# Interleaving the context products with the W products, and the products with A with the FFN products, in a gated cross-attention and FFN layer

## What is computed

```python
xn = layernorm(x);  xh, ch = heads(xn), heads(ctx)          # 4 heads of 128
Q, K, V = xh @ Wh, ch @ Wh, ch @ Wh                         # per head
scores = einsum("bshe,bthe->bhst", Q, K) / sqrt(128)
A = maximum(abs((scores * decay).sum(axis=0)), 1)           # summed over all 64 sequences
O = einsum("hst,bthe->bshe", A, V);  Y = groupnorm(O) * gamma + beta
x = x + tanh(g1) * ((relu(xn @ wg) * Y) @ wo)
h = layernorm(x)
x = x + tanh(g2) * ((silu(h @ gate.T * gs) * (h @ up.T * us)) @ down.T * ds)
```

## Time and profile before

| | |
|---|---|
| time, median of 3 runs | 1441.88 us |
| lowest, highest | 1441.26, 1445.92 us |
| span of the profiled execution (first to last instruction) | 1447.4 us |
| PE busy, of that span | 1420.4 us (98%) |
| DVE, ACT, POOL busy | 1043.3, 726.3, 735.3 us |
| mean granted TensorE clock | 0.998 of 2.4 GHz |
| first part, Z of group 1 to Z of group 15 | 34.1 to 311.7 us |
| FFN groups 0 to 7 | 360 to 1025 us |

### The profile page before, as it was taken

The page is one execution under the profiler, slowest core; times in us unless marked ns, Lnnn a source line. Parts: engine busy times, 40 slices in busy tenths (PEclk is TensorE's granted clock), DMA queues, the critical chain, the costliest instruction groups (busy, mean ns, idle before and its releaser), DMA issues.

```text
span 1447.4 us, 20320 instructions
## 1 busy us (share of the span) xinstructions
PE 1420.4 (98%) x7097; PEld 728.3 (50%) x7135; DVE 1043.3 (72%) x1562; ACT 726.3 (50%) x1145; POOL 735.3 (51%) x734
## 2 busy tenths in 40 slices
PE   8999999999999999999999999999999999999998
PEld 4666666665445544455444444444444444444443
DVE  7788998878477676766776677564867768768762
ACT  5566565554555635455463545534344444443442
POOL 5656769863564445444553554434137237137235
PEclk9999999999999999999999999999999999999999
DMA  8999898973878796987888897886383473572432
GB/s 275 344 336 306 292 317 318 343 251 130 276 204 263 227 276 206 260 276 210 248 274 237 264 243 222 247 252 164 112 228 115 124 224 122 139 218 98 139 109 89
DMA packets 372920, 324.96 MB, mean 225 GB/s; under 512 B 259280, under 2 KB 285264, under 8 KB 372816
## 3 DMA queue, kind: packets, MB, share of 16 engines
q1 hardware_dynamic: 355248, 291.63, 66.2%
q10 hardware_dynamic: 17568, 31.99, 6.2%
HBM read 209.14 MB, written 114.43 MB: 224 GB/s over the span
## 4 chain that ended last, share of the span: by engine, by line
PE 74%; DVE 10%; DMA 6%; SPq 3%; issue 3%; ACT 2%; POOL 2%; ACTq 0%; DVEq 0%; POOLq 0%
PE ps L2067 24%; PE po L2067 8%; PE pyb L1930 7%; PE ps L2074 7%; PE ptb L2074 5%; PE pyb L2074 5%; PE ps L1988 5%; PE po L1930 3%; PE pyb L2058 3%; PE ptb L2058 3%; DMA wy_scratch<-misc 2%; SPq L510 2%; DVE reg L1129 1%; PE ptb L2062 1%; PE pyb L2062 1%
## 5 line engine op out<-in xcount | busy, mean ns | idle before, releaser
L2067 PE MATMUL ps<-x2t,gate 128*128 128x512 f16 x704 | 166.6, 379 | 1.2 <-DVE tmp L1436 1.1
L1930 PE MATMUL pyb<-xnt,wgs 128*128 128x512 f16 x708 | 166.3, 380 | 1.4 <-DVE wgs L1153 1.3
L2067 PE MATMUL ps<-op,wbuf 128*128 128x512 f16 x704 | 166.3, 379 | 0.5 <-issue 0.5
L2067 PE MATMUL ps<-x2t,up 128*128 128x512 f16 x704 | 166.3, 379 | 0.0
L1800 POOL TENSOR_TENSOR p5b<-p5b,p1b 128x512 f32<-128x512 f32 x44 | 55.7, 1265 | 209.1 <-ACT p5b L860 209.1
L1816 POOL TENSOR_TENSOR hid<-tmp,hid 128x512 f16<-128x512 f32 x88 | 104.6, 1190 | 105.9 <-ACT hid L836 105.9
L2074 PE MATMUL ps<-down_first,hid 128*128 128x512 bf16 x683 | 152.4, 379 | 2.1 <-POOL hid L1816 0.8
L1811 POOL TENSOR_TENSOR hsp<-hall,hsp 128x640 f16<-128x640 f32 (+2 forms) x72 | 123.6, 1731 | 37.1 <-ACT hsp L887 37.1
L2067 PE MATMUL po<-op,wbuf 128*128 128x512 f16 x528 | 129.0, 379 | 0.6 <-DVE u2b L1383 0.6
L1436 DVE SCALAR_TENSOR_TENSOR tmp<-ps,colsb,tmp 128x512 f32<-128x512 f32 x88 | 65.4, 744 | 68.2 <-PE ps L2067 62.3
L1988 PE MATMUL ps<-reg 128*128 128x256 f32 x768 | 109.7, 294 | 4.3 <-DVE reg L1129 3.8
(11 more groups left out here) (218 smaller groups left out, 2764.2 us busy)
## 6 DMA issues: line engine op xcount, KB each, us to landing
wbuf<-ws_scratch SPq DMA_DIRECT2D x44, 896.0 KB, 5.0
xr<-in_x SPq DMA_DIRECT2D x62, 512.0 KB, 6.3
raw<-in_ctx_t SPq DMA_DIRECT2D x32, 512.0 KB, 5.6
v_scratch<-tmp ACTq DMA_DIRECT2D x64, 256.0 KB, 6.0
raw<-v_scratch SPq DMA_DIRECT2D x32, 512.0 KB, 6.6
x_scratch<-xr SPq DMA_DIRECT2D x32, 512.0 KB, 4.8
xr<-x_scratch SPq DMA_DIRECT2D x32, 512.0 KB, 5.9
raw<-w_scratch SPq DMA_DIRECT2D x31, 512.0 KB, 6.0
```

The lines of the kernel that those rows point to most:

```text
L1930: last = e.matmul(dst, lhs[a], rhs[b], start=(k == 0 and i == 0), stop=(k == n - 1 and i == 2))
L2067: last = e.matmul(dst, upper(wt), act[i], start=start, stop=stop and exact, skip_group_check=True)
```

## The change

In the first part the six matmuls of a half of v are followed, one by one, by six matmuls of a W tile. In groups 1 to 13 PE's order becomes v(4g, 0) alone, then v(4g+1, 0) with half of w(4g), v(4g, 1) with the other half, v(4g+1, 1) with half of w(4g+1), rows, v(4g+2, 0), v(4g+2, 1) and v(4g+3, 0) in the same way with the rest of w(4g+1) and with w(4g+2), and v(4g+3, 1) alone. Group 14 has three such halves. W tiles 4 to 56 with t % 4 under 2 go into the two `pz` banks, where Z has been. w(4g) therefore waits for z_lo(4g+2), w(4g+1) for z_lo(4g+3), and the next group's z for the w_out of these tiles. ACT's order is fitted to it. In the FFN's first eight groups the 12 matmuls of o(q), for q over 3 (28 pairs), each follow one of the first 12 matmuls of the step; their waits now stand at the step's start.

The numbers of matmuls, their operands, DVE's, POOL's and SP's programs and all DMAs stay the same in number and size.

```diff
         def pw(t):
+            if 4 <= t < LATE - 1 and t % 4 < 2:
+                return pz[t % 4]
             if t <= LATE:
                 return pyb[:, :]
...
(ACT, group g)
-                v_out(4 * g)
-                v_out(4 * g + 1)
+                if more and g < NG - 2:
+                    v_out(4 * g)
+                    w_out(4 * g)
+                    v_out(4 * g + 1)
...
                 ct_hi(g + 1, 1)
                 if g < NG - 2:
-                    w_out(4 * g)
+                    w_store(4 * g)
                 x_hi(2 * g + 3, 0)
-                if g < NG - 2:
-                    w_store(4 * g)
                 x_hi(2 * g + 3, 1)
+                w_out(4 * g + (1 if g < NG - 2 else 0))
                 v_out(4 * g + 2)
-                w_out(4 * g + (1 if g < NG - 2 else 0))
+                w_store(4 * g + (1 if g < NG - 2 else 0))
                 v_store(4 * g + 2)
-                v_out(4 * g + 3)
-                w_store(4 * g + (1 if g < NG - 2 else 0))
-                v_store(4 * g + 3)
+                ct_hi(g + 1, 2)
+                ct_hi(g + 1, 3)
...
(PE)
             def z(n):
...
+                if h < 2 and 8 <= n < LATE + 3:
+                    p.wait_ge("wev", n - 3)
...
-            def v(t, half):
+            def v(t, half, beside=None):
...
+                if beside:
+                    w_ready(*beside)
+                for n in range(6):
+                    h, (i, q) = 2 * half + n // 3, ((0, 0), (1, 0), (0, 1))[n % 3]
+                    last = e.matmul(ps[t % 2][:, h, :, :], ct[g % 2][i][:, h, 128 * b:128 * b + 128],
+                                    wh_and_z(q, h, b), start=(n % 3 == 0), stop=(n % 3 == 2))
+                    if half and n == 5:
+                        last.then_inc(s["v"])
+                    if beside:
+                        w_term(beside[0], beside[1][n // 3], n % 3)
...
+            def w_ready(t, ks):
                 x_ready(t // 4)
-                if 0 < t <= LATE:
+                if t in (1, 2, 3):
+                    p.wait_ge("wev", t)
+                elif 4 <= t < LATE - 1:
+                    p.wait_ge(*(("zlo", t + 3) if t % 4 < 2 else ("wev", t - 2) if t % 4 == 2 else ("wev", t)))
...
-            def up_mm(exact, g, j):
+            def up_mm(exact, g, j, beside=None):
+
+                n, m = 15 * g + j, 0
+                if beside:
+                    o_ready(beside)
...
+                        if beside and m < 12:
+                            o_term(beside, m)
...
                         for q, piece in pieces(15 * g + step):
                             if piece == 0 and q > 3:
-                                o(q)
+                                beside = q
...
(PE, group g)
-                if g > 1:
-                    rows(2 * g + 3)
-                if g < NG - 2:
-                    w(4 * g)
-                if g == 1:
-                    rows(5)
-                v(4 * g + 2, 0)
-                v(4 * g + 2, 1)
-                w(4 * g + (1 if g < NG - 2 else 0))
-                v(4 * g + 3, 0)
+                full = g < NG - 2
+                v(4 * g, 0)
+                v(4 * g + 1, 0, (4 * g, (0, 1)) if full else None)
+                v(4 * g, 1, (4 * g, (2, 3)) if full else None)
+                v(4 * g + 1, 1, (4 * g + 1, (0, 1)) if full else (4 * g, (0, 1)))
+                rows(5 if g == 1 else 2 * g + 3)
+                v(4 * g + 2, 0, (4 * g + 1, (2, 3)) if full else (4 * g, (2, 3)))
+                v(4 * g + 2, 1, (4 * g + 2, (0, 1)) if full else None)
+                v(4 * g + 3, 0, (4 * g + 2, (2, 3)) if full else (LATE - 1, (0, 1)))
                 v(4 * g + 3, 1)
```

More of the change, by code:

```diff
@@ L974, in _ @@
                     wo_sum(g - 3)
-                v_out(4 * g)
-                v_out(4 * g + 1)
+                if more and g < NG - 2:
+                    v_out(4 * g)
+                    w_out(4 * g)
+                    v_out(4 * g + 1)
+                else:
+                    v_out(4 * g)
+                    v_out(4 * g + 1)
                 v_store(4 * g)
@@ L990, in _ @@
                 if g < NG - 2:
-                    w_out(4 * g)
+                    w_store(4 * g)
                 x_hi(2 * g + 3, 0)
-                if g < NG - 2:
-                    w_store(4 * g)
                 x_hi(2 * g + 3, 1)
+                w_out(4 * g + (1 if g < NG - 2 else 0))
                 v_out(4 * g + 2)
-                w_out(4 * g + (1 if g < NG - 2 else 0))
+                w_store(4 * g + (1 if g < NG - 2 else 0))
                 v_store(4 * g + 2)
-                v_out(4 * g + 3)
-                w_store(4 * g + (1 if g < NG - 2 else 0))
-                v_store(4 * g + 3)
+                ct_hi(g + 1, 2)
+                ct_hi(g + 1, 3)
                 if 3 <= g < 7:
                     wo_hi(g - 3)
-                ct_hi(g + 1, 2)
-                ct_hi(g + 1, 3)
                 if g < NG - 2:
                     w_out(4 * g + 2)
+                v_out(4 * g + 3)
+                if g < NG - 2:
                     w_store(4 * g + 2)
+                v_store(4 * g + 3)
             w_out(LATE)
@@ L1923, in _, with three @@
             p = Program(e, s)
-            def three(dst, lhs, rhs, k, n, low=None):
+            def three(dst, lhs, rhs, k, n):
                 for i, (a, b) in enumerate(((0, 0), (0, 1), (1, 0))):
-                    if i == 2 and low:
-                        p.wait_ge(*low)
                     last = e.matmul(dst, lhs[a], rhs[b], start=(k == 0 and i == 0), stop=(k == n - 1 and i == 2))
@@ L1985, in v @@
                     p.wait_ge("acc", t - 1)
[L1986 to L1993, removed]
-                x_ready(t // 4)
-                if 0 < t <= LATE:
+                if beside:
[9 more added lines that the diff above has]
+            def w_ready(t, ks):
+                x_ready(t // 4)
+                if t in (1, 2, 3):
+                    p.wait_ge("wev", t)
+                elif 4 <= t < LATE - 1:
+                    p.wait_ge(*(("zlo", t + 3) if t % 4 < 2 else ("wev", t - 2) if t % 4 == 2 else ("wev", t)))
+                elif LATE - 1 <= t <= LATE:
                     p.wait_ge("wev", t)
@@ L2003, in w, with w_term, o_ready @@
                     p.wait_ge("vev", B)
-                for k in ks:
[L2005 to L2012, removed]
+            def w_term(t, k, i):
+                a, b = ((0, 0), (0, 1), (1, 0))[i]
+                if t == 0:
+                    p.wait_ge("scaledhi", k + 2)
+                    if a:
+                        p.wait_ge("scaledlo", k + 2)
+                last = e.matmul(pw(t), wgs[a][:, k, 128 * (t % 4):128 * (t % 4) + 128], xnt[t // 4 % 2][b][:, k, :],
+                                start=(k == 0 and i == 0), stop=(k == 3 and i == 2))
+                if k == 3 and i == 2:
+                    last.then_inc(s["w"])
+            def w(t, ks=range(4)):
+                w_ready(t, ks)
+                for k in ks:
+                    for i in range(3):
+                        w_term(t, k, i)
+            def o_ready(q):
                 p.wait_ge("vlo", q + 1)
@@ L2016, in o, with o_term @@
                     p.wait_ge("nr", 2 * q)
[L2017 to L2020, removed]
+            def o_term(q, n):
+                h, (a, b) = n // 3, ((0, 0), (0, 1), (1, 0))[n % 3]
+                last = e.matmul(po[:, h // 2, :, 128 * (h % 2):128 * (h % 2) + 128], a_parts[a][:, h, :],
+                                vs_of(q)[b][:, :, 128 * h:128 * h + 128], start=(n % 3 == 0), stop=(n % 3 == 2))
+                if n == 11:
+                    last.then_inc(s["o"])
+            def o(q):
+                o_ready(q)
+                for n in range(12):
+                    o_term(q, n)
             def y_t(t):
@@ L2107, in up_mm, with down_mm @@
                                          [x2t[0][:, k, :], x2t[1][:, k, :]], i, i == 0 and k == 0, i == 1 and k == 3)
-                    if i:
-                        last.then_inc(s[("gm", "um")[which]])
-            def down_mm(exact, g, t):
+                        if i and k == 3:
+                            last.then_inc(s[("gm", "um")[which]])
+                        if beside and m < 12:
+                            o_term(beside, m)
+                        m += 1
+            def down_mm(exact, g, t, beside=None):
                 n = 15 * g + 11 + t
+                if beside:
+                    o_ready(beside)
                 sl = slice(128 * t, 128 * t + 128)
@@ L2128, in down_mm @@
                                              done == 0, done == 2 * NI - 1)
+                            if beside and done < 12:
+                                o_term(beside, done)
                             done += 1
-                last.then_inc(s["dn"])
+                            if done == 2 * NI:
+                                last.then_inc(s["dn"])
             def half_sums(exact, w, *sums):
@@ L2213, in first_groups @@
```

(11 more changed lines are left out.)

6 lines of the change are left out of this document (1 added, 5 removed).

## The result

The changed kernel took 1485.68 us (median of 4 runs, 1485.04 to 1486.55) beside 1442.49 us for the kernel before (4 runs, 1441.26 to 1445.92): a ratio of 1.0298, 95% interval 1.0281 to 1.0315, 43 us slower. 1480 was forecast, with 1460 to 1498 around it.

What follows compares the result with a forecast made beforehand. It took PE to bound the kernel, with DVE a hair's breadth behind. DVE's loops 33.9, the groups around them 0.6 and the FFN 3.5 made 38.0 us on 1441.9: 1480 us, range 1460 to 1498.

Steps and rivals of the forecast that it cites:

- The matmuls: Interleaved products: an fp32r product with an f16 one behind it takes 0.131 us, against 0.120 in a run.
- The FFN's term: Products with A in the FFN: eleven more fp32r-to-f16 transitions in each of 28 pairs, +3.5 us.
- The bound of 0.108: Lower bound in us for an interleaved fp32r product, its weight load hidden; best case 9.9 us gained over 822 products.
- The loop: Twelve first-part loops through DVE: v_acc(4g+1) starts 7.0 us after z_lo(4g+2), not 3.1, so DVE waits; +33.9 us.
- The base: Carrying the span difference to the median: 38.0 us added to 1441.9, taking the median as 5.5 us below the span.
- Group 14: End of the first part: v_acc(57) comes 1.3 us later with DVE lightly loaded, +0.2 us.
- the rival of the falling clock: First part: PE's new waits lower the granted clock, 1 to 2.5 us in eight groups, 1488 to 1500 us; chance 0.14.
- the prediction's own signs of being wrong: DVE not idle ahead of v_acc(4g), a product pair of 0.324 us, or PE's clock below 1.00 in the first part.
- Loads hidden: Interleaved fp32r products cost 0.108 us as weight loads hide, while DVE's loop stays; 1466 us, chance 0.17.
- Transitions only: DVE finds its way without the new waits and only the dearer matmuls count: 9 us, 1451 us; chance 0.05.
- Faster: Weight loads hidden at all 822 products and DVE's loop not binding: up to 9.9 us gained, 1432 to 1434; chance 0.07.

Runs made afterwards that it cites:

- the pair of fitted kernels: fit_products and fit_sixes: changed first part, FFN of the kernel before, DVE's order fitted to PE's; 1461.2 and 1458.7 us.
- first_only: The changed kernel with o(q) ahead of the FFN step again, so only the first part is changed; 1481.0 us, ratio 1.0266.
- ffn_only: The kernel before with only the products with A interleaved with the FFN products, first part untouched; 1449.3 us, ratio 1.0041.
- fit_sixes: As fit_products, but six fp32r products and then six f16 products instead of product by product; 1458.7 us, ratio 1.0107.
- fit_products: dve_order with the FFN of the kernel before and stats(4g+7) moved behind the next group's z_lo; 1461.2 us, ratio 1.0125.
- dve_order: The changed kernel with only DVE's order changed: low_weights and wo_lo or wg_top moved into its gaps around v_acc; 1465.0 us, ratio 1.0154.
- two edits: Each on the changed kernel: six W products behind each six of v, 1477.3 us; w(4g) written to pyb again, 1479.1 us.

## Why the prediction was right

The direction, the place and the mechanism were right: DVE, with its program unedited, waits for a v_out that comes later, and its lateness comes back to PE. Of the sizes, some were right by luck.

**The matmuls.** 0.131 was taken for an fp32r product with an f16 one behind it, from the one transition in the trace. It is 0.134, and 0.0147 over one in a run by the pair of fitted kernels. The row had said as much: 0.35 less 0.216 is 0.134, and the prediction wrote 0.13. The FFN's term, 3.5 us, measured 4.6 and 4.8 in the traces and 4.7 and 6.4 between medians. The bound of 0.108 on the other side was never near.

**The loop.** 7.0 us to v_acc(4g+1) measured 7.09, and 33.9 us as the difference of the profiled executions measured 33.6 (273.9 less 240.3). That the sum met to 0.3 us is luck, for two errors cancelled in it. DVE's waits for v_out in the loops were 62.4 us, not 57.4: 2.3 of the 5 us are at v_acc(4g+3), which waited 6.3 us in all where 4.0 were forecast, and most of the rest is at v_acc(4g) and v_acc(4g+1). Another 1.0 us is a wait for a load. Against that everything else on DVE took 210.5 us, not 216.8; `wo_lo` in groups 4 to 7 is 3.8 us of the difference (below), and the rest isn't broken down. So group 5, forecast at 23.6 us, took 23.1: `wo_lo` is 1.1 us shorter there and v_acc(23) comes 0.6 later.

**The base.** 38 was forecast and 43 came between medians, but only 36.0 between the two profiled spans (1483.4 less 1447.4). The step that was short is the one that carried the difference of the spans over to the median, with the base's own waits in it. The changed kernel's profiled execution has a span of 1483.4 and a time of 1485.4, so 2.0 us lie around the span. By that the profiled execution of before took some 1449.4 us, 7 above its median. It has the wait of 2.77 us at 772 and the slow matmuls behind it, which the same FFN in first_only has not (659.0 us against 664.2), and its loops are 1.8 us longer than those of ffn_only. Against such executions the loops cost 35.4 us, the FFN 4.6, and the stretch from z_lo(58) to the FFN another 1.8: 41.8 in all, near the 43. The loop's term was 1.5 us short by this, the FFN's 1.1 and that of group 14 1.6.

**Group 14.** Behind z_lo(58) it was forecast at +0.2 us and cost 1.8. PE waits there for a w_out, for which the prediction counted nothing:

```profile
345.89 0.35 PE L1997 MATMUL ps<-reg 128*128 128x256 f32 x1 [1.64 <-ACT tmp L745]
```

By the code this is w(57), which is written to `pyb` but waits for w_out(56), although w(56) now stands in a `pz` bank. `w_ready` kept the old wait there. No run takes it out.

**The clock.** At the start of group 14, still inside the last loop, PE waited 3.5 us at z(58) for z_lo(56), behind group 13 with its scale factors, and the granted clock was 0.51 behind it:

```profile
333.20:336.20 3.00, 2.99 (x8) 1.07 (x9) 3.00 (x6) 0.80 (x2) 2.92 (x2) 0.51 0.50 201
```

That is the rival of the falling clock, at one place of the first part, and one of the prediction's own signs of being wrong. The six Z products took 2.74 us there, and 1.47 elsewhere. It didn't come in groups 4 to 9: the waits of 1.4 to 1.8 us at z(4g+6) left the clock at 1.00. At the start of group 11 the two kernels with this first part differ. In the changed kernel a wait of 2.84 us left the clock at 1.00, in first_only the same wait of 2.74 us was followed by 0.63 over 3.9 us. So the length of the wait alone doesn't decide here.

**The rivals.** Loads hidden: refuted by the pair of 0.350 us and by fit_sixes against fit_products. Transitions only: refuted by first_only and dve_order. Faster: refuted; even with DVE's loop mostly open (fit_products) a group in which PE hardly waits is 0.45 us longer than before. The edit of DVE's order brings back 20.6 of 43 us, the undo of the FFN's part 4.7 to 6.4. Some 10 to 15 us in the loops of the fitted kernels stay, of which the transitions are 5.3 in fit_products (12 times 0.44). What the rest of the first part would need, a place for the scale factors, wasn't tried.

## What to carry to other kernels

Before PE's order is changed, write down for each engine that waits for it what it can do between its waits. An engine busy 90% of a group with an order written out by hand is tied to the old order, and a result that comes 4 us later costs it some 3 us in every group although its work is the same. Look for every such result: here a second one, at v_acc(4g+3), took about half of what two edits were to gain. A gain per matmul is to be read at both transitions, into the other kind of product and out of it: the second one decided here. And a difference of two spans is added to a median only after it is asked which waits of the profiled execution the other executions have.

## What the runs showed of the hardware

`wo_lo`, one DVE instruction of 128x512 with three operands in SBUF, took 1.39 to 1.84 us in the kernel before and 0.74 in the changed one. Its duration (min/median/max ns) in the one and in the other:

```profile
L1245 DVE SCALAR_TENSOR_TENSOR wos<-up,wo_lim,wos x4: 1389/1783/1840, 115.0 to 176.4; 128x512 f16<-128x512 f32 x4
```

```profile
L1251 DVE SCALAR_TENSOR_TENSOR wos<-up,wo_lim,wos x4: 740/742/742, 125.4 to 194.2; 128x512 f16<-128x512 f32 x4
```

In the kernel before, POOL ran its 512-column subtractions beside it:

```profile
134.29 2.50 POOL L1721 TENSOR_TENSOR reg<-raw,reg 128x512 fp32r<-128x512 f32 x2 [1.54 <-ACT reg L706]
136.77 0.65 POOL L1688 TENSOR_SCALAR rs<-mv 128x2 f32<-128x2 f32 x1
```

In the changed kernel it stood beside POOL's small instructions, or behind the last subtraction. In the kernel before each of the four ends 0.54 to 0.56 us after the end of the subtraction that it met, wherever it had begun. The shortest is the one that began furthest into it:

```profile
176.41 1.39 DVE L1245 SCALAR_TENSOR_TENSOR wos<-up,wo_lim,wos 128x512 f16<-128x512 f32 x1
```

```profile
174.74 2.50 POOL L1721 TENSOR_TENSOR reg<-raw,reg 128x512 fp32r<-128x512 f32 x2 [1.37 <-ACT reg L706]
```

So 0.55 of its 0.74 us of work came behind POOL's instruction. DVE's `TENSOR_REDUCE` beside the same subtractions kept its 0.88 us. dve_order and fit_products bear it out: all four took 0.74 to 0.75 us in the one, where POOL had nothing long beside them, and two took 1.48 in the other, where it had. Where `wo_lo` begins first it is POOL that is slow: in ffn_only one began at 136.91 and took 0.74 us, and the subtraction that began beside it, at 136.99, took 1.8 us in place of 1.25. Why is not shown, and no run tries it by itself.

An f16 weight load doesn't start with the fp32r matmul ahead of it but 0.12 us later, in every pair looked at. An fp32r load does start beside an f16 matmul, and beside an fp32r one too: in a run such loads last 0.19 us each and the matmuls follow every 0.120 us.
